# Joint rounding of h and x, three scale instructions moved to ScalarE, and a new VectorE order in a linear-attention + FP4 feed-forward block

## Chip, cores and metric

One core of one Trainium2 chip. The metric is device time in microseconds of one execution (lower is better); the time of a kernel is the median over its runs.

## What is computed

x is (8, 2048, 256), so 16384 tokens of 256 values. With xn = layernorm(x), the output is x + attention(xn) + ffn(xn).

```python
qkv = xn @ W_qkv.T                       # 16 heads of 16
q = softmax(q, axis=-1) * 16 ** -0.5;  k = exp(k)
# buckets of 64 tokens; context and sum of k are cumulated over the buckets before
attn = einsum(q, context) / max(einsum(q, ksum), 1e-6)
attention = attn @ W_out.T

def fp4_quant_dequant(v):                # blocks of 16 along the last axis
    scale = maximum(max(abs(v)) / 6, 1e-12)
    return GRID[searchsorted(MID, abs(v / scale))] * sign(v) * scale
gate = q4(xn) @ q4(w_gate).T;  y = q4(xn) @ q4(w_up).T      # 704 columns
ffn = q4(silu(gate) * y) @ q4(w_down).T
```

## The kernel before, in words

A tile is 128 rows: two buckets of 64 tokens. There are 128 tiles, four sequences of 32. Every engine has its own instruction list, written out by hand, in a function `step(n, d)`: step k = 2n + d does pieces of several tiles at once, and the order of the calls in `step` is the order of the work on that engine. Engines wait for each other, and VectorE for its own results, with counting semaphores (`wait_ge`).

**TensorE** in step k (`step` at the end of its block): the qkv projection of tile k+1; the transpose of attention of k-1; the attention numerator and the context sum (`bucket`) of k; a matmul that subtracts the high half of the attention from its transpose (`less_att`); gate and up of k, first half of the 704 columns (`gate_up(k, 0)`, twelve matmuls of 352 columns); the transpose of xn of k+2 (L1041); six matmuls of `gate_up(k, 1)`; `less_xn` of k+2 (L1049); six more of `gate_up(k, 1)`; the transpose of exp(q) of k+1 (L1073); the output projection of k-2 and the down projection of k-2 (`project_h`, 17 matmuls). `gate_up(k, 1)` writes the PSUM banks in which the qkv product of k+1 stood, so it waits until VectorE has subtracted q's maximum there (`q_shift`) and ScalarE has read k and v (`kv_done`). `less_xn` waits for ScalarE's first copy of the transposed xn (`xnt_split`).

**ScalarE** in step k: first copy of the transposed attention; exp(k) and v of k+1; second copy of the attention; exp(q) of k+1 (`exp_q`, L534, waits for `q_shift`); tanh of the first gate half (L558); first copy of the transposed xn (`split_xnt`, L513); second copy; tanh of the second half; layernorm's normalise of k+3, mean and squares of k+4; copy of the transposed q; eight snapshot copies of the context (L573).

**VectorE** in step k: the last two products of x's quantization for tile k+1 (`scale_x`, L874 and L876, which feed a DMA transpose that SyncE issues); block maxima of x (k+2) and h (k-1); `block_scales` with eleven short instructions, among them two reciprocals, of 16 (x) and 44 (h) block scales, and the high and low halves of the scales; `max_q`; h divided by its scales (`over_scales_h`, L807); `shift_q` (L697); the two residual additions of tile k-3 (`add_up`); between them the three rounding instructions of h (L825, L829, L835) and x's division (L816); the gate products (L734, L744); x's three rounding instructions (L843, L847, L853) spread over the second half; the attention's four short steps (L710, L714, L718, L723); the last two products of h (`scale_h`, L863), which feed the other DMA transpose; `row_factor` (L883, L888). A value is rounded in three instructions: the upper 16 bits of the fp32 quotient with the lowest bit set, a multiplication by a power of two into fp16, and an addition and subtraction on those 16 bits.

h and x have quotient, rounding and scale buffers of their own. POOL computes 1/std of the layernorm. SyncE issues the loads, the stores and the DMA transposes, in a written order (`turn_xq`, `turn_h`, `load`, `store`).

```python
nc.tensor.matmul(tr32, minus16[:, :], xnt[:, par, 0, :], start=False, stop=True, ...)   # less_xn, after
pe.wait_ge(xnt_split, after(t, 2, 1))
...
elif 0 in chunks:                                # gate_up(t, 1)
    pe.wait_ge(q_shift, after(t + 1))
    pe.wait_ge(kv_done, after(t + 1, 3))
```

Of the kernel before, what the change touches and what calls it, by code (L numbers as in the profile page):

```python
# [5 lines left out]
def linear_attention_fp4_ffn_block(nc, x, wqkv_t, wout_t, wgate, wup, wdown, out):  # L6
# [18 lines left out]
    P = 128  # L25
# [41 lines left out]
    with ctx:  # L67
# [74 lines left out]
        xv = sb("xv", [P, D])  # L142
        xw = sb("xw", [P, D], u16)
        xu = sb("xu", [P, D], fp16)
        xq = sb("xq", [P, D], u16)
# [5 lines left out]
        hblk = sb("hblk", [P, 3, FB])  # L151
# [4 lines left out]
        hv = sb("hv", [P, F])  # L156
        hw = sb("hw", [P, F], u16)
        hu = sb("hu", [P, F], fp16)
        hq = sb("hq", [P, F], u16)
# [55 lines left out]
        xq_round = sem("xq_round")  # L215
# [10 lines left out]
        c_row_done = sem("c_row_done")  # L226
        proj_done = sem("proj_done")
# [36 lines left out]
        def _(sp):  # L264
# [35 lines left out]
            def turn_xq(t, par):  # L300
                if not is_tile(t):
                    return
                sp.wait_ge(xq_step, after(t, 8))
                sp.sem_inc(sp_turn, 1)
                if begun(t - 2):
                    sp.wait_ge(gu_done, after(t - 2, 2))
                sp.sem_inc(sp_turn, 1)
                sp.dma_start_transpose(xqt[:, par, :, :].rearrange("p s (c k) -> p (s c) k", k=P),
                                       xq_s[:, par, :, :].rearrange("p s k -> p (s k)")).then_inc(xqt_done[par], 16)

            def turn_h(t, par):
                if not is_tile(t):
                    return
                sp.wait_ge(hq_step, after(t, 14))
# [127 lines left out]
        def _(act):  # L442
# [49 lines left out]
            def normalise_waits(t):  # L492
# [5 lines left out]
                if begun(t - 2):  # L498
                    act.wait_ge(xq_step, after(t - 2, 8, 6))
# [60 lines left out]

            def snapshot(t):
# [14 lines left out]
            def step(n, d):  # L576
# [4 lines left out]
                exp_q(k + 1, odd)  # L581
                tanh_gate(k, 0, par)
# [4 lines left out]
                tanh_gate(k, 1, par)  # L587
                normalise(n, d + 3)
# [41 lines left out]
        def _(dve):  # L630
# [107 lines left out]
            def times_up(t, half, par):  # L738
# [3 lines left out]
                if begun(t - 2):  # L742
                    dve.wait_ge(hq_step, after(t - 2, 14, 8))
# [17 lines left out]
            def block_scales(t, par, u, upar):  # L761

                do_h, do_x = is_tile(t), is_tile(u)
                if do_x:
                    dve.wait_ge(xq_step, after(u, 8, 1))
                    nc.vector.tensor_scalar(xblk[:, 1, :], xblk[:, 0, :], SIX_TIE * 2.0 ** 11, XS * TINY * 2.0 ** 11, ALU.mult, ALU.max)\  # L769
                        .then_inc(xq_step, 1)  # L770
                if do_h:
                    dve.wait_ge(hq_step, after(t, 14, 1))
                    nc.vector.tensor_scalar(hblk[:, 1, :], hblk[:, 0, :], SIX_TIE, h_floor[:, :], ALU.mult, ALU.max)\
                        .then_inc(hq_step, 1)
                if do_x:
                    dve.wait_ge(xq_step, after(u, 8, 2))
                    nc.vector.reciprocal(xblk[:, 2, :], xblk[:, 1, :]).then_inc(xq_step, 1)  # L777
                if do_h:
                    dve.wait_ge(hq_step, after(t, 14, 2))
                    nc.vector.tensor_reduce(hrow[:, 0, :], hblk[:, 1, :], AX.X, ALU.max).then_inc(hq_step, 1)  # L780
                if do_h:
                    nc.vector.reciprocal(hblk[:, 2, :], hblk[:, 1, :]).then_inc(hq_step, 1)
                    dve.wait_ge(hq_step, after(t, 14, 3))
                    nc.vector.tensor_scalar(hrow[:, 1, :], hrow[:, 0, :], 2.0 ** -23, None, ALU.mult)\
                        .then_inc(hq_step, 1)
                if do_x:
                    nc.vector.tensor_copy(xs_hi[:, :].rearrange("p (b i) -> p b i", i=2), twice(xblk[:, 1, :])).then_inc(xq_step, 1)
                if do_h:
                    dve.wait_ge(hq_step, after(t, 14, 5))
                    nc.vector.reciprocal(hrow[:, 2, :], hrow[:, 1, :]).then_inc(hq_step, 1)  # L790
                if do_x:
                    dve.wait_ge(xq_step, after(u, 8, 4))
                    nc.vector.tensor_tensor(xs_lo[:, :].rearrange("p (b i) -> p b i", i=2), twice(xblk[:, 1, :]),
                                            xs_hi[:, :].rearrange("p (b i) -> p b i", i=2), ALU.subtract).then_inc(xq_step, 1)
                if do_h:
                    dve.wait_ge(hq_step, after(t, 14, 6))
                    nc.vector.tensor_scalar(hs_hi[:, :].rearrange("p (b i) -> p b i", i=2), twice(hblk[:, 1, :]), hrow[:, 2, :], None, ALU.mult)\
                        .then_inc(hq_step, 1)

            def over_scales_h(t, par):  # L800
                if not is_tile(t):
                    return
                dve.wait_ge(hq_step, after(t, 14, 4))
                if begun(t - 1):
                    dve.wait_ge(hq_step, after(t - 1, 14, 9))
                rows = lambda ap: ap.rearrange("p (o b i) -> p o b i", b=FB, i=2)
                nc.vector.tensor_tensor(rows(hv[:, :]), rows(h[:, par, :]), pairs_of(hblk[:, 2, :]), ALU.mult)\  # L807
                    .then_inc(hq_step, 1)

            def over_scales_x(t, par):  # L810
                if not is_tile(t):
                    return
                dve.wait_ge(xq_step, after(t, 8, 3))
                if begun(t - 1):
                    dve.wait_ge(xq_round, after(t - 1, 3, 1))
                nc.vector.tensor_tensor(xv[:, :].rearrange("p (o b i) -> p o b i", b=XB, i=2),  # L816
# [3 lines left out]
            def round_h(t, part):  # L820
                if not is_tile(t):
                    return
                if part == 0:
                    dve.wait_ge(hq_step, after(t, 14, 8))
                    nc.vector.tensor_scalar(hw[:, :], hv[:, :].bitcast(u16)[:, 1:2 * F:2], 1, None, ALU.bitwise_or)\  # L825
                        .then_inc(hq_step, 1)
                if part == 1:
                    dve.wait_ge(hq_step, after(t, 14, 9))
                    nc.vector.tensor_scalar(hu[:, :], hw[:, :].bitcast(bf16), 2.0 ** -14, None, ALU.mult)\  # L829
                        .then_inc(hq_step, 1)  # L830
                if part == 2:
                    dve.wait_ge(hq_step, after(t, 14, 10))
                    if begun(t - 1):
                        dve.wait_ge(hq_step, after(t - 1, 14))
                    nc.vector.tensor_scalar(hq[:, :], hu[:, :].bitcast(u16), GRID16, -GRID16, ALU.add, ALU.add)\  # L835
                        .then_inc(hq_step, 1)

            def round_x(t, part):
                if not is_tile(t):
                    return  # L840
                if part == 0:
                    dve.wait_ge(xq_step, after(t, 8, 6))
                    nc.vector.tensor_scalar(xw[:, :], xv[:, :].bitcast(u16)[:, 1:2 * D:2], 1, None, ALU.bitwise_or)\  # L843
                        .then_inc(xq_round, 1)
                if part == 1:
                    dve.wait_ge(xq_round, after(t, 3, 1))
                    nc.vector.tensor_scalar(xu[:, :], xw[:, :].bitcast(bf16), 2.0 ** -3, None, ALU.mult)\  # L847
                        .then_inc(xq_round, 1)
                if part == 2:
                    dve.wait_ge(xq_round, after(t, 3, 2))  # L850
                    if begun(t - 1):
                        dve.wait_ge(xq_step, after(t - 1, 8))
                    nc.vector.tensor_scalar(xq[:, :], xu[:, :].bitcast(u16), GRID16, -GRID16, ALU.add, ALU.add)\  # L853
                        .then_inc(xq_round, 1)

            def scale_h(t, par, part):
# [3 lines left out]
                dve.wait_ge(hq_step, after(t, 14, 12))  # L860
                if begun(t - 2):
                    dve.wait_ge(hqt_done[par], turned(t - 2, par))
                nc.vector.tensor_tensor(rows(hq_s[:, par, part * F:(part + 1) * F]), rows(hq[:, :].bitcast(fp16)),  # L863
                                        over_pairs((hs_hi, hs_lo)[part][:, :]), ALU.mult).then_inc(hq_step, 1)

            def scale_x(t, par):
# [3 lines left out]
                dve.wait_ge(xq_round, after(t, 3))  # L870
                dve.wait_ge(xq_step, after(t, 8, 5))
                if begun(t - 2):
                    dve.wait_ge(xqt_done[par], turned(t - 2, par))
                nc.vector.tensor_tensor(rows(xq_s[:, par, 0, :]), rows(xq[:, :].bitcast(fp16)), over_pairs(xs_hi[:, :]), ALU.mult)\  # L874
                    .then_inc(xq_step, 1)
                nc.vector.tensor_tensor(rows(xq_s[:, par, 1, :]), rows(xq[:, :].bitcast(fp16)), over_pairs(xs_lo[:, :]), ALU.mult)\  # L876
                    .then_inc(xq_step, 1)

            def row_factor(t, par):
                if not is_tile(t):  # L880
                    return
                dve.wait_ge(hq_step, after(t, 14, 7))
                nc.vector.scalar_tensor_tensor(hs_lo[:, :].rearrange("p (b i) -> p b i", i=2), twice(hblk[:, 1, :]), hrow[:, 2, :],  # L883
                                               hs_hi[:, :].rearrange("p (b i) -> p b i", i=2), ALU.mult,
                                               ALU.subtract).then_inc(hq_step, 1)
                if begun(t - 2):
                    dve.wait_ge(o_step, after(t - 2, 2))
                nc.vector.tensor_scalar(c_row[:, par, :], hrow[:, 1, :], c_d[:, :], None, ALU.mult)\  # L888
# [374 lines left out]
```

## Time and profile before

| | |
|---|---|
| median of 3 runs | 1497.29 us (1495.11 to 1497.63) |
| profiled execution, its own time | 1495.11 us |
| its span, first to last instruction | 1493.3 us |
| granted TensorE clock, mean | 0.988 |
| instructions: TensorE / VectorE / ScalarE / POOL | 10702 / 4914 / 3096 / 540 |

The span is read in three parts: about 110 us in which the weights are quantized and transposed and the first steps run, the steady stretch of some 125 steps, and a drain of some 25 us. "Busy" of an engine counts the time in which an instruction of it runs; two neighbours may overlap, since the next one starts before the last one's end. The distance from start to start is therefore what an instruction costs its engine.

### The profile page before, as it was taken

The numbers are of one execution on the slowest core, as the hardware profiler recorded it, in microseconds if no ns is written. First come the engines' busy times: TensorE is split into PE (matmuls) and PEld (weight loads), VectorE is DVE, ScalarE is ACT, GpSimd is POOL, SyncE is SP. The second block draws the span as 40 slices with busy tenths as digits, with TensorE's granted clock in tenths as the row PEclk, the third lists the DMA queues.
The fourth block names the chain that finished last, engine by engine and source line by source line (L and its number), as shares of the span: only waits on it lengthen the run. The fifth ranks groups of instructions, "written<-read, shape, count | busy, mean of one in ns | idle before, by whom it ended". The sixth has DMA issues, their size and how long they took to land.

```text
span 1493.3 us, 43457 instructions
## 1 busy us (share of the span) xinstructions
PE 1382.8 (93%) x10702; PEld 948.7 (64%) x10702; DVE 1434.4 (96%) x4914; ACT 1011.0 (68%) x3096; POOL 175.8 (12%) x540
## 2 busy tenths in 40 slices
PE   0259999999999999999999999999999999999997
PEld 0136666666666666666666666666666666666664
DVE  5859999999999999999999999999999999999997
ACT  1687767676767677676767676767767676767662
POOL 1520101010101101010101010110101010101000
PEclk9969999999999999999999999999999999999998
DMA  5002233333332333333333323333333333233324
GB/s 114 4 7 55 63 65 77 69 63 74 70 76 58 81 68 70 64 81 68 63 71 74 72 58 78 68 70 64 81 68 69 65 77 71 61 73 70 71 47 78
DMA packets 293241, 100.01 MB, mean 67 GB/s; under 512 B 258272, under 2 KB 292704, under 8 KB 293216
## 3 DMA queue, kind: packets, MB, share of 16 engines
q1 hardware_dynamic: 293216, 99.73, 31.8%
q8 instruction: 9, 0.15, 0.0%
q14 instruction: 16, 0.13, 0.0%
HBM read 19.99 MB, written 16.78 MB: 25 GB/s over the span
## 4 chain that ended last, share of the span: by engine, by line
DVE 53%; issue 34%; DVEq 7%; ACT 3%; PE 1%; SPq 1%; DMA 0%; POOL 0%; ACTq 0%; POOLq 0%
DVE q_rows L863 5%; DVE osum L900 4%; DVE hw L825 4%; DVE xblk L758 3%; DVE h L744 3%; DVE xw L843 2%; DVE hu L829 2%; DVE hq L835 2%; DVE hv L807 2%; DVE xq_s L876 2%; DVE att L723 1%; DVE xblk L777 1%; DVE qsh L697 1%; DVE hs_lo L883 1%; DVE xblk L769 1%
## 5 line engine op out<-in xcount | busy, mean ns | idle before, releaser
L1154 PE MATMUL outp<-w_down_cat,q_rows 128*128 128x256 f16 x1408 | 246.2, 274 | 0.0
L573 ACT ACTIVATE snap<-ctxp,mask 64x68 f32<-64x68 f32 x1024 | 236.2, 308 | 3.2
L550 ACT ACTIVATE att_t<-trp 128x256 f16<-128x256 f32 x256 | 98.3, 384 | 134.0 <-PE trp L1109 129.6
L534 ACT ACTIVATE qexp<-qsh,c_q 128x256 f32<-128x256 f32 x128 | 65.1, 508 | 147.4 <-DVE qsh L697 147.3
L398 POOL TENSOR_TENSOR var_scaled<-squares,var_mul 128x1 f32<-128x1 f32 x128 | 24.8, 194 | 1188.4 <-ACT scratch L488 1181.7
L1154 PEld LDWEIGHTS outp<-w_down_cat,q_rows 128*128 128x128 f16 x1408 | 138.3, 98 | 16.5
L1156 PE MATMUL outp<-w_down_lo,q_rows 128*128 128x256 f16 x640 | 147.6, 274 | 0.0
L513 ACT ACTIVATE xnt<-trp 128x256 f16<-128x256 f32 x256 | 96.8, 378 | 57.3 <-PE trp L1049 57.3
L751 DVE TENSOR_REDUCE hblk<-h 128x44 f32<-128x704 f32 x128 | 123.6, 966 | 0.1
L807 DVE TENSOR_TENSOR hv<-h,hblk 128x704 f32<-128x704 f32 x128 | 112.7, 881 | 0.0
L558 ACT ACTIVATE th<-unit1a,c_g 128x352 f32<-128x352 f32 x128 | 69.7, 545 | 36.3 <-PE unit1b L1027 36.3
L1087 PE MATMUL nump<-snap,qt 128*64 128x144 f32 x1024 | 91.0, 299 | 3.2 <-ACT snap L573 3.2
L558 ACT ACTIVATE th<-unit0a,c_g 128x352 f32<-128x352 f32 x128 | 69.8, 545 | 29.7 <-PE unit0b L1027 29.7
L1041 PE MATMUL trp<-ident,xn 128*128 128x128 f32 x256 | 49.4, 275 | 37.7 <-ACT xn L504 37.7
L1023 PE MATMUL unit0a<-w_gate,xqt 128*128 128x352 f16 x256 | 80.5, 315 | 3.4 <-DVE qsh L697 1.2
L1023 PE MATMUL unit1a<-w_gate,xqt 128*128 128x352 f16 x256 | 80.5, 314 | 2.9
L504 ACT ACTIVATE xn<-xring,shift,rstd 128x256 f32 (+1 forms) x128 | 75.3, 589 | 11.1 <-POOL shift L408 11.1
L1023 PE MATMUL unit1b<-w_up,xqt 128*128 128x352 f16 x256 | 80.0, 313 | 0.0
L1025 PE MATMUL unit1b<-w_up,xqt 128*128 128x352 f16 x256 | 80.0, 313 | 0.0
L1023 PE MATMUL unit0b<-w_up,xqt 128*128 128x352 f16 x256 | 80.0, 313 | 0.0
L1027 PE MATMUL unit1b<-w_up,xqt 128*128 128x352 f16 x256 | 80.0, 313 | 0.0
L1027 PE MATMUL unit0a<-w_gate,xqt 128*128 128x352 f16 x256 | 80.0, 313 | 0.0
(214 smaller groups left out, 4409.2 us busy)
## 6 DMA issues: line engine op xcount, KB each, us to landing
xring<-x SPq DMA_DIRECT2D x128, 128.0 KB, 2.7
out<-xring SPq DMA_DIRECT2D x128, 128.0 KB, 2.5
xqt<-xq_s SPq DMA_TRANSPOSE x128, 2.4
q_rows<-q_rows SPq DMA_TRANSPOSE x128, 3.5
raw_qkv<-wqkv_t SPq DMA_DIRECT2D x1, 768.0 KB, 7.7
raw_gate<-wgate SPq DMA_DIRECT2D x8, 88.0 KB
raw_up<-wup SPq DMA_DIRECT2D x8, 88.0 KB
raw_down<-wdown SPq DMA_DIRECT2D x1, 704.0 KB, 6.2
```

Of the source, the lines that this page charges most:

```text
L513: nc.scalar.activation(xnt[:, par, part, :], tr32, ACT.Copy).then_inc(xnt_split, 1)
L550: nc.scalar.activation(att_t[:, par, part, :], tr32, ACT.Copy).then_inc(att_split, 1)
L558: nc.scalar.activation(th[:, half, :], unit[(par + half) % 2][0][:, 0:FH], ACT.Tanh, scale=c_g[:, :])\
L573: nc.scalar.activation(kept[:, :, cols], sums[:, :, cols], ACT.Copy, scale=mask[rows, f, h:h + 1])\
L751: nc.vector.tensor_reduce(hblk[:, 0, :], h[:, par, :].rearrange("p (o b i) -> p b o i", b=FB, i=2), AX.XY, ALU.max, apply_absolute_value=T ...
L807: nc.vector.tensor_tensor(rows(hv[:, :]), rows(h[:, par, :]), pairs_of(hblk[:, 2, :]), ALU.mult)\
L1023: nc.tensor.matmul(o, stat_hi, m, start=first, stop=False)
L1025: nc.tensor.matmul(o, stat_hi, m, start=False, stop=False)
L1027: end = nc.tensor.matmul(o, stat_lo, m, start=False, stop=last)
L1087: last = nc.tensor.matmul(nump[rows, g * 2 * SW:(g + 1) * 2 * SW], qt[:, par, g * P + s * BUCKET:g * P + (s + 1) * BUCKET], snap[:, g, s, ...
L1154: nc.tensor.matmul(downp, hqt[:, par, m, :], w_down_cat[:, m, :], start=(m == 0), stop=False)
L1156: nc.tensor.matmul(downp, hqt[:, par, m, :], w_down_lo[:, m, :], start=False, stop=False)
```

## The change

The scale, quotient and rounding buffers of h and x are laid side by side (`blk` of 44 + 16 columns, `hx_v`, `hx_w`, `hx_u`, `hx_q` of 704 + 256), so that one reciprocal and three rounding instructions serve both. The powers of two in h's scales are changed so that one factor fits both. The high halves of both scales (`xs_hi`, `hs_hi`) and the row factor (`c_row`) are computed on ScalarE: the first two between `exp_q` and the first `tanh_gate`, the last behind the second `tanh_gate`. On VectorE, `max_q` moves ahead of the row maximum and the reciprocal, `shift_q` ahead of the row scale's reciprocal and h's division, and x's division stands directly behind h's.

```diff
-        xblk = sb("xblk", [P, 3, XB])
+        blk = sb("blk", [P, 3, FB + XB])
+        hblk, xblk = blk[:, :, 0:FB], blk[:, :, FB:FB + XB]
...
+            def scales_x(t):                       # ScalarE
+                act.wait_ge(xq_step, after(t, 6, 2))
+                nc.scalar.activation(xs_hi[:, :].rearrange("p (b i) -> p b i", i=2), twice(xblk[:, 1, :]), ACT.Copy)\
+                    .then_inc(x_scaled, 1)
+            def factor_of_row(t, par):
+                act.wait_ge(hq_step, after(t, 9, 4))
+                if begun(t - 2):
+                    act.wait_ge(o_step, after(t - 2, 2))
+                nc.scalar.activation(c_row[:, par, :], hrow[:, 1, :], ACT.Copy, scale=c_d[:, :]).then_inc(c_row_done, 1)
+            def scales_h(t):
+                act.wait_ge(hq_step, after(t, 9, 5))
+                nc.scalar.activation(hs_hi[:, :].rearrange("p (b i) -> p b i", i=2), twice(hblk[:, 1, :]), ACT.Copy,
+                                     scale=hrow[:, 2, :]).then_inc(h_scaled, 1)
...
                 exp_q(k + 1, odd)
+                scales_x(k + 2)
+                scales_h(k - 1)
                 tanh_gate(k, 0, par)
...
                 tanh_gate(k, 1, par)
+                factor_of_row(k - 1, odd)
                 normalise(n, d + 3)
...
+            def over_one(t, u):                    # VectorE: row maximum, joined reciprocal
+                    nc.vector.tensor_reduce(hrow[:, 0, :], hblk[:, 1, :], AX.X, ALU.max).then_inc(hq_step, 1)
+                    nc.vector.reciprocal(blk[:, 2, both], blk[:, 1, both]).then_inc(hx_step, 1)
+            def round_hx(t, u, part):
+                both = slice(0 if do_h else F, F + D if do_x else F)
+                if part == 0:
+                        dve.wait_ge(hq_step, after(t, 9, 6))
+                        dve.wait_ge(xq_step, after(u, 6, 3))
+                    nc.vector.tensor_scalar(hx_w[:, both], hx_v[:, both].bitcast(u16)[:, 1:2 * (both.stop - both.start):2], 1, None,
+                                            ALU.bitwise_or).then_inc(hx_step, 1)
...
+            def low_scales(t, u):                  # waits for x_scaled and h_scaled, then xs_lo and hs_lo
...
                 block_max_h(k - 1, odd)
-                block_scales(k - 1, odd, k + 2, par)
+                block_scales(k - 1, k + 2)
                 max_q(k + 1, odd)
+                over_one(k - 1, k + 2)
+                row_scale(k - 1)
+                shift_q(k + 1, odd)
+                over_row(k - 1)
                 over_scales_h(k - 1, odd)
-                shift_q(k + 1, odd)
+                over_scales_x(k + 2, par)
+                round_hx(k - 1, k + 2, 0)
                 add_up(n, d - 3, 0)
-                round_h(k - 1, 0)
-                over_scales_x(k + 2, par)
-                round_h(k - 1, 1)
+                round_hx(k - 1, k + 2, 1)
                 add_up(n, d - 3, 1)
-                round_h(k - 1, 2)
+                round_hx(k - 1, k + 2, 2)
                 gate_h(k, 0, par)
-                row_factor(k - 1, odd)
-                round_x(k + 2, 0)
+                low_scales(k - 1, k + 2)
                 times_up(k, 0, par)
-                round_x(k + 2, 1)
                 attention(k, par, 0)
                 scale_h(k - 1, odd, 0)
+                attention(k, par, 1)
                 scale_h(k - 1, odd, 1)
-                round_x(k + 2, 2)
-                attention(k, par, 1)
                 attention(k, par, 2)
```

`row_scale` also waits for `c_row_done` of the tile before, because ScalarE now reads `hrow`. The rows that ScalarE and SyncE wait for are renumbered; SyncE's order is the same.

## Rows read from the trace of the kernel before

**Rows 1.** Steady stretch: busy us (xcount) of PE, PEld, DVE, ACT, POOL; clock, DMA, GB/s.
```profile
200.00:1450.00 1250.00, 1236.78 (x9604) 849.42 (x9602) 1244.39 (x4407) 874.18 (x2779) 131.59 (x460) 1.00 0.33 70
```

**Rows 2.** VectorE groups by shape, 200 to 1450 us: count, busy us, mean ns, idle.
```profile
L807 DVE TENSOR_TENSOR hv<-h,hblk 128x704 f32<-128x704 f32 x116 | 102.2, 881 | 0.0
L825 DVE TENSOR_SCALAR hw<-hv 128x704 uint16<-128x704 uint16 x116 | 59.6, 514 | 0.0
L782 DVE RECIPROCAL hblk<-hblk 128x44 f32<-128x44 f32 x116 | 48.5, 418 | 0.0
L829 DVE TENSOR_SCALAR hu<-hw 128x704 f16<-128x704 bf16 x116 | 38.7, 334 | 0.0
L843 DVE TENSOR_SCALAR xw<-xv 128x256 uint16<-128x256 uint16 x116 | 32.4, 279 | 0.0
L797 DVE TENSOR_SCALAR hs_hi<-hblk,hrow 128x88 bf16<-128x88 f32 x116 | 30.9, 266 | 0.0
L777 DVE RECIPROCAL xblk<-xblk 128x16 f32<-128x16 f32 x116 | 28.5, 246 | 0.0
L847 DVE TENSOR_SCALAR xu<-xw 128x256 f16<-128x256 bf16 x116 | 25.1, 217 | 0.0
L888 DVE TENSOR_SCALAR c_row<-hrow,c_d 128x1 f32<-128x1 f32 x116 | 23.7, 204 | 0.0
L787 DVE CAST xs_hi<-xblk 128x32 bf16<-128x32 f32 x116 | 20.0, 172 | 0.0
```

**Rows 3.** VectorE in one step, in order of time: start us, duration us, engine, line.
```profile
813.75 0.42 DVE L697 TENSOR_TENSOR qsh<-unit1b,qmax 128x256 f32<-128x256 f32 x1
814.08 0.47 DVE L900 SCALAR_TENSOR_TENSOR osum<-outp,c_o,xring 128x256 f32<-128x256 f32 x1
...
818.77 0.16 DVE L714 SCALAR_TENSOR_TENSOR dmx<-dz,nump 128x16 f32<-128x16 f32 x1
818.96 0.25 DVE L718 RECIPROCAL drec<-dmx 128x16 f32<-128x16 f32 x1
```

**Rows 4.** TensorE in the same step, in order of time.
```profile
808.57 0.39 PE L1023 MATMUL unit1a<-w_qkv,xnt 128*128 128x512 f16 x1
...
810.53 0.38 PE L1109 MATMUL trp<-ident,att 128*128 128x128 f32 x2
...
813.86 0.38 PE L1041 MATMUL trp<-ident,xn 128*128 128x128 f32 x2
814.30 0.32 PE L1023 MATMUL unit1a<-w_gate,xqt 128*128 128x352 f16 x1
...
815.05 0.31 PE L1027 MATMUL unit1b<-w_up,xqt 128*128 128x352 f16 x1
815.48 0.28 PE L1049 MATMUL trp<-xnt,minus 128*128 128x256 f16 x1
...
816.50 0.38 PE L1073 MATMUL trp<-ident,qexp 128*128 128x128 f32 x2
816.71 0.27 PE L1023 MATMUL outp<-w_out,att_t 128*128 128x256 f16 x1
...
819.42 0.39 PE L1023 MATMUL unit0a<-w_qkv,xnt 128*128 128x512 f16 x1
```

**Rows 5.** ScalarE in the same step, in order of time.
```profile
812.60 0.38 ACT L550 ACTIVATE att_t<-trp 128x256 f16<-128x256 f32 x1
814.20 0.51 ACT L534 ACTIVATE qexp<-qsh,c_q 128x256 f32<-128x256 f32 x1 [1.22 <-DVE qsh L697]
814.62 0.53 ACT L558 ACTIVATE th<-unit0a,c_g 128x352 f32<-128x352 f32 x1
815.05 0.37 ACT L513 ACTIVATE xnt<-trp 128x256 f16<-128x256 f32 x1
...
816.77 0.56 ACT L558 ACTIVATE th<-unit1a,c_g 128x352 f32<-128x352 f32 x1 [0.53 <-PE unit1b L1027]
...
819.02 1.87 ACT L573 ACTIVATE snap<-ctxp,mask 64x68 f32<-64x68 f32 x8
```

More of the change, by code:

```diff
@@ L788, in block_scales @@
[L788 to L798, printed above, removed]
+            def over_row(t):
+                if not is_tile(t):
+                    return
+                dve.wait_ge(hq_step, after(t, 9, 4))
+                nc.vector.reciprocal(hrow[:, 2, :], hrow[:, 1, :]).then_inc(hq_step, 1)
@@ L859, in scale_h @@
                 rows = lambda ap: ap.rearrange("p (o c) -> p o c", c=2 * FB)
[L860 to L863, printed above, removed]
+                if part == 0:
+                    dve.wait_ge(hx_step, hx_after(t + 3, 4))
+                    if begun(t - 2):
+                        dve.wait_ge(hqt_done[par], turned(t - 2, par))
+                else:
+                    dve.wait_ge(hq_step, after(t, 9, 7))
+                nc.vector.tensor_tensor(rows(hq_s[:, par, part * F:(part + 1) * F]), rows(hx_q[:, 0:F].bitcast(fp16)),
                                         over_pairs((hs_hi, hs_lo)[part][:, :]), ALU.mult).then_inc(hq_step, 1)
@@ L869, in scale_x @@
                 rows = lambda ap: ap.rearrange("p (o c) -> p o c", c=2 * XB)
-                dve.wait_ge(xq_round, after(t, 3))
-                dve.wait_ge(xq_step, after(t, 8, 5))
+                dve.wait_ge(hx_step, hx_after(t, 4))
+                dve.wait_ge(xq_step, after(t, 6, 4))
                 if begun(t - 2):
                     dve.wait_ge(xqt_done[par], turned(t - 2, par))
-                nc.vector.tensor_tensor(rows(xq_s[:, par, 0, :]), rows(xq[:, :].bitcast(fp16)), over_pairs(xs_hi[:, :]), ALU.mult)\
+                nc.vector.tensor_tensor(rows(xq_s[:, par, 0, :]), rows(hx_q[:, F:F + D].bitcast(fp16)), over_pairs(xs_hi[:, :]), ALU.mult)\
@@ L875, in scale_x @@
                     .then_inc(xq_step, 1)
-                nc.vector.tensor_tensor(rows(xq_s[:, par, 1, :]), rows(xq[:, :].bitcast(fp16)), over_pairs(xs_lo[:, :]), ALU.mult)\
+                nc.vector.tensor_tensor(rows(xq_s[:, par, 1, :]), rows(hx_q[:, F:F + D].bitcast(fp16)), over_pairs(xs_lo[:, :]), ALU.mult)\
                     .then_inc(xq_step, 1)
[L879 to L888, printed above, removed]
-                    .then_inc(c_row_done, 1)
+            def low_scales(t, u):
+                if is_tile(u):
+                    dve.wait_ge(x_scaled, after(u))
+                    nc.vector.tensor_tensor(xs_lo[:, :].rearrange("p (b i) -> p b i", i=2), twice(xblk[:, 1, :]),
+                                            xs_hi[:, :].rearrange("p (b i) -> p b i", i=2), ALU.subtract).then_inc(xq_step, 1)
+                if is_tile(t):
+                    dve.wait_ge(h_scaled, after(t))
+                    nc.vector.scalar_tensor_tensor(hs_lo[:, :].rearrange("p (b i) -> p b i", i=2), twice(hblk[:, 1, :]), hrow[:, 2, :],
+                                                   hs_hi[:, :].rearrange("p (b i) -> p b i", i=2), ALU.mult,
+                                                   ALU.subtract).then_inc(hq_step, 1)
```

126 lines of the change are left out of this document (56 added, 70 removed).

## The prediction

> **What bounds the kernel now.** I read the busy times by stretch first. Between 200 and 1450 us VectorE is busy 1244 of 1250 us, TensorE 1237 at a granted clock of 1.00 (its level of 2.4 GHz), ScalarE 874 [rows 1]. The reader should see two full engines, not one. Next come VectorE's groups: each stands there 116 times [rows 2], so a step takes 1250 / 116 = 10.78 us, and no group has idle time before it. VectorE is the bound. TensorE's busy time is misleading, since durations overlap; its slack has to be found in the distances from start to start.
>
> So the third view is the timeline of TensorE for one step, 808.57 to 819.42, 10.85 us [rows 4]. It has two places in which more time passes than the work needs. (a) The transpose of xn starts at 813.86 and the next matmul, first of `gate_up(k, 1)`, at 814.30: 0.44 us. The same pair of transposes followed by an fp16 matmul takes 0.21 at 816.50. The wait in between is for `shift_q`, which ends at 813.75 + 0.42 = 814.17 [rows 3]. (b) Six gate matmuls run from 814.30, five distances of (815.05 - 814.30) / 5 = 0.15; `less_xn` should follow 0.15 behind the last, but starts 0.43 behind it, at 815.48. ScalarE's copy that it waits for ends at 815.05 + 0.37 = 815.42 [rows 5]. So 0.23 + 0.28 = 0.51 of this step is waiting, and TensorE's own step is 10.85 - 0.51 = **10.34 us**. I looked at some eighty steps: both waits are in every one, smaller in the neighbouring step, which is also shorter. Both go back to VectorE: (a) directly, (b) because ScalarE's exp(q) waited 1.22 us for the same `shift_q`, and tanh and the copy stand behind it [rows 5].
>
> The timeline is therefore: VectorE 10.78, TensorE 10.34 close behind it, ScalarE 874 / 116 = 7.5. Whatever VectorE loses beyond 0.44 us a step cannot show.
>
> **The change, part by part: VectorE.** An independent instruction starts before its predecessor ends: L697 takes 0.42 and the next starts 0.33 behind it, so an instruction costs its duration less 0.09. One that needs the result right in front of it costs more: L714 takes 0.16 and L718 starts 0.19 behind it [rows 3], 0.12 above the rule.
> - Moved to ScalarE: `xs_hi` 172 ns, `hs_hi` 266, `c_row` 204 [rows 2]. 0.64 - 3 x 0.09 = 0.37 us saved.
> - Reciprocals: 418 ns for 44 columns, 246 for 16, so 6.1 ns a column; 60 columns take 418 + 98 = 516. Two cost 0.66 - 0.18 = 0.48, one 0.43: 0.05 saved.
> - First rounding instruction: 514 ns for 704 columns, 279 for 256, 0.52 a column; 960 columns take 649. 0.61 becomes 0.56: 0.05. The second: 334 and 217, so 401 for 960; 0.37 becomes 0.31: 0.06. The third, of the same width on 16-bit data, I price like the second: 0.06.
> - L718 gets h's second product between it and L714: 0.12 saved. But the joined first rounding stands directly behind x's division, whose result it needs: 0.12 lost. The other moved instructions each keep a neighbour between them and their source.
> Sum: 0.37 + 0.05 + 0.05 + 0.06 + 0.06 = **0.59 us saved**; VectorE then needs 10.78 - 0.59 = 10.19 a step. Bounds: the joined instructions could save nothing (0.37), or each save the whole fixed part, about 0.2 as the 16-column reciprocal suggests, instead of 0.05 (1.0). I keep the slopes, since both widths of each form are in the trace.
>
> **TensorE.** `shift_q` now stands ahead of h's division (881 - 90 = 0.79) and the high scales are out (0.08 + 0.18), so relative to the rest of the step it ends at least 1.05 earlier, at 813.1 instead of 814.17. Gap (a) closes whole: `gate_up(k, 1)` could start at 814.07. Bounds of (a): 0.21 left as at 816.50, or all of 0.44 as now, if the other waits of that call or the change from fp32 to fp16 cost it. I take 0.21, because that row is the same pair of instructions followed by an fp16 matmul.
>
> **ScalarE**, in offsets from TensorE's first matmul of the step (808.57). Its second attention copy is done at 4.41 (812.60 + 0.38). exp(q) started at 5.63 and can now start at about 4.6; it holds the engine 0.42 (814.20 to 814.62), so until 5.0. The two new copies, 32 and 88 columns wide, have no row of their own; the nearest are the snapshot copies, 68 columns with a per-partition scale, 1.87 / 8 = 0.23 each [rows 5]. Two end at 5.47. The bounds are 0.2 and 0.8 for the two. tanh cannot start before the gate is in PSUM anyway: the second half's starts 0.27 behind the first transpose that follows the gate (816.50 to 816.77), so the first half's can start at 5.29 + 0.27 = 5.56 at the earliest. **The copies fit into that wait, with 0.09 to spare.** Then tanh 0.43, the xn copy 0.37, done at 6.36; the matmul starts 0.06 later (815.42 to 815.48), at 6.42. TensorE is there at 5.29 + 0.21 + 6 x 0.15 = 6.40. Of (b) 0.02 stays. If the copies took 0.8 instead of 0.47, 0.24 more would stay.
>
> The ScalarE page of the Trainium skill, "ScalarE: Activation LUTs", section "Rules for kernel authors", speaks against this move: simple multiplications belong on VectorE, which is faster by the element. In the same page's figures (186 ns and 0.833 a column, 93 more for a scale read from memory, 93 of overlap) I estimate 0.12 and 0.26 for the two copies, 0.38 in all, and the stay of (b) would be as above, 0.02. The rule is about the cost of one operation; here the operation goes where there is a wait.
>
> The row factor behind the second tanh costs about 0.2 in front of normalise. ScalarE's step, counted to the end of the snapshots, ended 820.89, 1.47 into TensorE's next step; with the shorter step and the extra work it ends at about 1.7, before the numerator matmuls behind the transpose at 810.53 - 808.57 = 1.96 need it. `c_row` of a tile is used two steps later, and VectorE's wait for it before the next row scale is some 5 us behind it. `low_scales` waits for copies done at 5.5, and comes at about 7. I cost these at nothing; the cover of the low scales is 1.5 us.
>
> **Who waits now.** TensorE's step is 10.34 + 0.02 = 10.36, VectorE's 10.19. VectorE runs ahead until `max_q` has to wait for the qkv product, which ends at about 2.1; that is its new idle place, 0.17 a step. POOL, SyncE and the DMA transposes keep their order and their slack.
>
> **Sum.** 10.78 - 10.36 = 0.42 us, in 125 steps: 52 us. The drain has no x and little TensorE work; there VectorE saves the moved instructions, 0.37 in three steps: 1 us. The start is kept. The profiled execution, 1495.1 (span 1493.3 and 1.8 around it), becomes 1442; it is 2.2 below the median of the runs shown, so a median is some 2 us above that. I give **1443 us**.
>
> **The rivals.**
> 1. *Gap (a) is not VectorE's* (0.14). It stays at 0.44. TensorE's step is 10.59, 0.19 saved, 24 us: 1471. For it: the call has two more waits than the one at 816.71. Against it: the matmul starts 0.13 behind `shift_q`'s end, as one that was released by it would.
> 2. *TensorE is no floor* (0.04). Then all of VectorE's 0.59 shows: 125 x 0.59 = 74, so 1421. Against it: the matmuls stand 0.15 apart with no wait between them. The page "TensorE: Matmul & The Clock Gate", section "Back-to-back issue gap", would have it so: it gives 131 ns for a matmul of 512 columns in a sustained stream of weight loads and matmuls. The trace disagrees: 0.15 for 352 columns. By that page TensorE would have room and the time would be the 1421 of this rival.
> 3. *ScalarE's copies come late* (0.06, the slower side). Place: between exp(q) and the first tanh. Each 0.1 us in which they hold tanh beyond 5.56 delays `less_xn`, and so the step, by 0.1. The point at which it decides is a step of 10.78, so copies (with their wait for the reciprocal of the row scale, which stands behind `shift_q`) of 0.47 + 0.09 + 0.42 = 0.98 us. At 1.3 us the step is 11.1: 125 x 0.32 = 40 slower, 1537. Against: no row of ScalarE shows a short copy above 0.31, and the reciprocal is done 0.25 behind `shift_q`, while exp(q) runs.
> 4. *Nothing changes* (0.03): VectorE meets new waits on ScalarE, as long as what it saves. 1497. Against: 1.5 us of cover.
> 5. *As forecast* (0.73), 1434 to 1454: 0.1 us of a step either way is 12 us.
>
> **How the numbers follow.** The likeliest case gives 1443. The range reaches down to 1431 (the gap behind the transpose shrinks to the plain distance of 0.15, 7 us, and a little of the start) and up to 1473, which takes in rival 1, and copies at their bound of 0.8 us (0.24 a step, 30 us: also 1473); it leaves out rivals 2, 3 and 4, 0.13 together, and what lies beyond their neighbours' bounds. A measurement of this kernel tells 0.2%, 3 us, from no change. Faster: cases 5, 1, 2, less a little, 0.91; the same 0.03; slower 0.06.
>
> **What would show it.** Right: VectorE has idle time in front of `max_q`, released by the qkv matmuls, of about 0.17 us a step; TensorE's distance behind the xn transpose is 0.21 and in front of `less_xn` about 0.17; exp(q) starts right behind the attention copy and waits no more; the step is 10.36. Wrong: `less_xn` still 0.3 or more behind its predecessor with ScalarE as releaser (rival 3), the 0.44 kept with `shift_q` long done (rival 1), VectorE without idle time (I mis-sized it).

## The result, and the profile after

| | before | changed |
|---|---|---|
| median | 1497.39 us (4 runs, 1495.11 to 1497.63) | 1443.53 us (4 runs, 1442.89 to 1445.99) |
| ratio | | 0.9644, 95% interval 0.963 to 0.9659 |
| span of the profiled execution | 1493.3 | 1441.8 |

Forecast were 1443 and a range of 1431 to 1473. The busy times in the steady stretch of the changed kernel, the row that answers to [rows 1]:

```profile
200.00:1400.00 1200.00, 1200.00 (x9600) 856.04 (x9599) 1163.06 (x3595) 936.88 (x3125) 135.32 (x460) 1.00 0.34 73
```

TensorE is busy all of the 1200 us, VectorE 1163. A step takes 1200 / 116 = 10.345 us; it took 10.78. (Averaged from start to start over more than 100 steps: 10.355, and 10.784 before. The difference of 0.43 is the same.) The chain of work that ended last was mostly VectorE and "issue" before; now the page of the profile gives it to TensorE:

```profile
PE 91%; ACT 3%; DVE 2%; issue 1%; ACTq 0%; DVEq 0%
```

TensorE in one step of the changed kernel, in order of time, the rows that answer to [rows 4]:

```profile
805.80 0.39 PE L1032 MATMUL unit1a<-w_qkv,xnt 128*128 128x512 f16 x1
...
807.76 0.38 PE L1118 MATMUL trp<-ident,att 128*128 128x128 f32 x2
...
811.09 0.38 PE L1050 MATMUL trp<-ident,xn 128*128 128x128 f32 x2
811.31 0.31 PE L1032 MATMUL unit1a<-w_gate,xqt 128*128 128x352 f16 x1
...
812.05 0.31 PE L1036 MATMUL unit1b<-w_up,xqt 128*128 128x352 f16 x1
812.25 0.28 PE L1058 MATMUL trp<-xnt,minus 128*128 128x256 f16 x1
...
815.98 0.28 PE L1166 MATMUL outp<-w_down_lo,q_rows 64*128 64x256 f16 x1
816.20 0.39 PE L1032 MATMUL unit0a<-w_qkv,xnt 128*128 128x512 f16 x1
```

The gap behind the transpose of xn (811.09 to 811.31) is 0.22; it was 0.44. The one in front of the subtraction (812.05 to 812.25) is 0.20 here and 0.15 in the neighbouring step; 0.43 and 0.32 before. On average over all steps the first went from 0.44 to 0.22 and the second from 0.37 to 0.175.

ScalarE in the same step, the answer to [rows 5], with the two new copies (L563, L578) and the row factor (L572):

```profile
809.83 0.38 ACT L548 ACTIVATE att_t<-trp 128x256 f16<-128x256 f32 x1
810.11 0.50 ACT L532 ACTIVATE qexp<-qsh,c_q 128x256 f32<-128x256 f32 x1
810.51 0.22 ACT L563 ACTIVATE xs_hi<-blk 128x32 bf16<-128x32 f32 x1
810.63 0.36 ACT L578 ACTIVATE hs_hi<-blk,hrow 128x88 bf16<-128x88 f32 x1
811.37 0.55 ACT L556 ACTIVATE th<-unit0a,c_g 128x352 f32<-128x352 f32 x1 [0.38 <-PE unit0b L1036]
811.82 0.38 ACT L511 ACTIVATE xnt<-trp 128x256 f16<-128x256 f32 x1
...
814.00 0.28 ACT L572 ACTIVATE c_row<-hrow,c_d 128x1 f32<-128x1 f32 x1
```

exp(q) follows the attention copy at once; it waited 1.22 us. tanh still waits, now for the gate matmuls, 0.38 us behind the copies.

VectorE's waits and groups, 200 to 1400 us (first the view of waits: total, times, longest; then groups):

```profile
DVE qmax L711 <- PE unit0b L1036: 20.7, 58, 0.4
DVE qmax L711 <- PE unit1b L1036: 10.3, 55, 0.3
```
```profile
L848 DVE TENSOR_SCALAR hx_w<-hx_v 128x960 uint16<-128x960 uint16 x116 | 76.5, 660 | 4.0
L806 DVE RECIPROCAL blk<-blk 128x60 f32<-128x60 f32 x116 | 60.0, 517 | 0.0
L757 DVE SCALAR_TENSOR_TENSOR ga<-th,unit0a 128x352 f32<-128x352 f32 x116 | 56.2, 485 | 0.0
L852 DVE TENSOR_SCALAR hx_u<-hx_w 128x960 f16<-128x960 bf16 x116 | 46.3, 399 | 0.0
L860 DVE TENSOR_SCALAR hx_q<-hx_u 128x960 uint16<-128x960 uint16 x116 | 46.2, 398 | 0.0
```

VectorE is now idle in front of `max_q`, released by the qkv matmuls, as forecast, and for longer: 31.0 / 116 = 0.27 us a step by this view. By distances it is 0.35, because `max_q` usually starts 0.08 to 0.09 before its predecessor ends: the distance in front of it averages 0.51, where without a wait it is 0.16 (experiments 2 and 7). So VectorE's own need, the time that its instructions of one step take when it waits for no other engine, is 10.345 - 0.35 = **9.99 us**, TensorE's **10.345**. Its slack, what it can lose before the step gets longer, is the 0.35. (With the averaged step it is 10.355 - 0.35 = 10.00. The expectations use 9.99 and 10.345.)

### The profile page after: what moved, and what is told of

Its sections match the earlier page's. It is cut to its first block, busy times and chain, and to the rows that moved or that the text cites. A ratio compares the mean times of both kernels' runs of the same rounds, so it can differ in the third digit from the quotient of the medians.

```text
span 1441.8 us, 42471 instructions
## 1 busy us (share of the span) xinstructions
PE 1342.2 (93%) x10702; PEld 955.3 (66%) x10702; DVE 1342.9 (93%) x4030; ACT 1081.1 (75%) x3480; POOL 179.9 (12%) x540
## 4 chain that ended last, share of the span: by engine, by line
PE 91%; ACT 3%; DVE 2%; issue 1%; ACTq 0%; DVEq 0%
PE outp L1163 11%; PE nump L1096 6%; PE unit1a L1032 5%; PE unit0a L1032 5%; PE outp L1165 5%; PE unit1a L1034 5%; PE unit1a L1036 5%; PE unit0a L1034 4%; PE unit0a L1036 4%; PE ctxp L1106 4%; PE unit1b L1034 4%; PE unit1b L1032 4%; PE unit1b L1036 4%; PE unit0b L1036 4%; PE unit0b L1032 4%; PE unit0b L1034 4%
## 5 line engine op out<-in xcount | busy, mean ns | idle before, releaser
L396 POOL TENSOR_TENSOR var_scaled<-squares,var_mul 128x1 f32<-128x1 f32 x128 | 34.4, 269 | 1134.0 <-ACT scratch L486 1126.3
L774 DVE TENSOR_REDUCE blk<-h 128x44 f32<-128x704 f32 x128 | 123.8, 968 | 0.1
L827 DVE TENSOR_TENSOR hx_v<-h,blk 128x704 f32<-128x704 f32 x128 | 111.5, 871 | 0.0
L848 DVE TENSOR_SCALAR hx_w<-hx_v 128x960 uint16<-128x960 uint16 (+2 forms) x131 | 84.9, 648 | 4.9
L1034 PE MATMUL unit1b<-w_up,xqt 128*128 128x352 f16 x256 | 80.0, 313 | 0.0
L1036 PE MATMUL unit0b<-w_up,xqt 128*128 128x352 f16 x256 | 80.0, 313 | 0.0
L1032 PE MATMUL unit0b<-w_up,xqt 128*128 128x352 f16 x256 | 80.0, 313 | 0.0
L1034 PE MATMUL unit0b<-w_up,xqt 128*128 128x352 f16 x256 | 80.0, 313 | 0.0
```

The source lines that it names most:

```text
L774: nc.vector.tensor_reduce(hblk[:, 0, :], h[:, par, :].rearrange("p (o b i) -> p b o i", b=FB, i=2), AX.XY, ALU.max, apply_absolute_value=T ...
L827: nc.vector.tensor_tensor(rows(hx_v[:, 0:F]), rows(h[:, par, :]), pairs_of(hblk[:, 2, :]), ALU.mult)\
L1032: nc.tensor.matmul(o, stat_hi, m, start=first, stop=False)
L1034: nc.tensor.matmul(o, stat_hi, m, start=False, stop=False)
L1036: end = nc.tensor.matmul(o, stat_lo, m, start=False, stop=last)
```

## The experiments

Theory A, the prediction's, sharpened by that profile: a step takes the larger of TensorE's 10.345 and VectorE's need, and the change lowers the second from 10.78 to 9.99. Rivals: B, the early subtraction of q is what ends TensorE's waits; C, the other parts are each needed; D, TensorE is no bound; E, VectorE still is the bound; F, ScalarE's copies are on the path.

**1. q late, rest kept.**

```diff
-                max_q(k + 1, odd)
                 over_one(k - 1, k + 2)
                 row_scale(k - 1)
-                shift_q(k + 1, odd)
+                max_q(k + 1, odd)
                 over_row(k - 1)
                 over_scales_h(k - 1, odd)
+                shift_q(k + 1, odd)
```

> The changed kernel with q's maximum and subtraction put back where they stood (maximum behind the row scale, subtraction behind h's division); everything else of the change stays. Theory A (VectorE now has 0.27 us of idle time a step and TensorE is the bound, so the order of q is no longer needed): 1443 to 1446 us, TensorE's step still 10.35. q's subtraction ends 0.3 us later in TensorE's step, still before ScalarE is free for exp(q). Theory B (the early subtraction is what ends TensorE's waits): both waits come back, 0.1 to 0.3 us a step, 1455 to 1480.

Measured: 1443.77 us (1442.95 to 1447.02). Theory B falls: both of TensorE's gaps are as in the changed kernel, 0.22 and 0.175 on average. With VectorE below TensorE's need it is ahead by itself, and q's subtraction is early enough at either place.

**2. Scales and row factor back on VectorE.**

```diff
-                scales_x(k + 2)                    # ScalarE
-                scales_h(k - 1)
...
-                factor_of_row(k - 1, odd)
...
                 row_scale(k - 1)                   # VectorE
+                high_x(k + 2)
                 shift_q(k + 1, odd)
...
+                high_h(k - 1)
                 gate_h(k, 0, par)
                 low_scales(k - 1, k + 2)
+                factor_of_row(k - 1, odd)
```

> The changed kernel with the three scale instructions back on VectorE (0.09 + 0.19 + 0.12 = 0.40 us a step); joined rounding and q's order stay. Theory A: VectorE needs 10.07 + 0.40 = 10.47 us a step, over TensorE's 10.35, becomes the bound again, and the time rises by 0.12 x 125 = 15 us to 1459 (1450 to 1470). Theory C (the gain is in the order and the joined instructions): no change, 1443.

Measured: 1444.14 us (1444.1 to 1446.52). This is the number that C, as the expectation words it, had; A's missed by 15 us. I had set VectorE's need from the idle time (0.27), not from the distance (0.35). With 9.99 + 0.38 = 10.37 it is level with TensorE: its step averages 10.38, and it has no wait in front of `max_q` any more. Taken alone, the run cannot tell A, so corrected, from C; experiments 3, 4 and 5 do. In VectorE's timeline the three instructions cost 0.09, 0.17 and 0.12 (806.71 to 806.80, 810.44 to 810.61, 811.37 to 811.49):

```profile
806.71 0.17 DVE L866 CAST xs_hi<-blk 128x32 bf16<-128x32 f32 x1
806.80 0.42 DVE L695 TENSOR_TENSOR qsh<-unit1b,qmax 128x256 f32<-128x256 f32 x1
...
810.44 0.26 DVE L871 TENSOR_SCALAR hs_hi<-blk,hrow 128x88 bf16<-128x88 f32 x1
810.61 0.52 DVE L732 SCALAR_TENSOR_TENSOR ga<-th,unit0a 128x352 f32<-128x352 f32 x1
...
811.37 0.21 DVE L878 TENSOR_SCALAR c_row<-hrow,c_d 128x1 f32<-128x1 f32 x1
811.49 0.51 DVE L742 TENSOR_TENSOR h<-ga,unit0b 128x352 f32<-128x352 f32 x1
```

**3. Not joined.**

```diff
-                    nc.vector.reciprocal(blk[:, 2, both], blk[:, 1, both]).then_inc(hx_step, 1)
+                    for s in parts:                # slice(0, FB), slice(FB, FB + XB)
+                        nc.vector.reciprocal(blk[:, 2, s], blk[:, 1, s]).then_inc(hx_step, 2 // len(parts))
...
```
The three rounding instructions are parted in the same way, with the waits in front of them unchanged.

> The changed kernel with separate instructions for h and x in the reciprocal and the three rounding steps (same places). By the slopes VectorE pays 0.06 + 3 x 0.06 = 0.25 us more a step, and gets 0.12 back, since x's division no longer stands directly in front of an instruction that needs it. Theory A: 0.13 fits into the idle 0.27, so 1443 to 1445. Theory C (the joining is needed): 0.25 a step, 1470.

Measured: 1444.02 us (1442.83 to 1444.88), as A had it. The 0.12 that the expectation gave back did not come: this kernel still waits for x's division in front of the first rounding instruction of h, and the distance behind that division is 0.45, as in the changed kernel. By distances the parting costs 0.22, and 9.99 + 0.22 still lies below TensorE's step.

**4. Only the moves to ScalarE** (edits 1 and 3 together).

> Of the change only the three instructions moved to ScalarE (and the places of x's rounding and the attention's short steps): separate instructions for h and x, q's maximum and subtraction late as before. Theory A: VectorE needs 10.2 to 10.35 us a step, at or below TensorE's 10.35: 1443 to 1450. Theory B or C (the other parts carry the gain): 1465 or more.

Measured: 1444.74 us (1444.56 to 1447.78). One part of the change gives its whole time, to within some 1 us. The buffers' new layout and the new places are still in this kernel; the three moves on the otherwise unchanged kernel before were not run.

**5. Only the order** (edits 2 and 3 together).

> The changed kernel with both other parts undone: the three scale instructions on VectorE and separate instructions for h and x; q's early subtraction and the new places stay. Counted in distances from start to start, VectorE needs 9.99 us a step in the changed kernel (10.345 less 0.35 in front of q's maximum). Theory A (VectorE's need against TensorE's 10.345): 9.99 + 0.38 + 0.26 - 0.12 = 10.51, so 0.165 x 125 = 21 us more, 1464 (1455 to 1475). Theory B (q's early subtraction is what ends TensorE's waits): 1444 to 1450.

Measured: 1473.21 us (1470.51 to 1474.83). Theory A's 1464 is 9 us off, inside its range. Now VectorE is over the line. The step below takes 10.54, read between the same instruction in two steps,

```profile
804.33 0.73 DVE L826 TENSOR_SCALAR hx_w<-hx_v 128x704 uint16<-128x704 uint16 x2
...
814.42 0.41 DVE L810 TENSOR_TENSOR hx_v<-xn,blk 128x256 f32<-128x256 f32 x1
814.87 0.53 DVE L826 TENSOR_SCALAR hx_w<-hx_v 128x704 uint16<-128x704 uint16 x1
```

but the steps differ, and over 105 of them the average is 10.60. That is 0.245 above the changed kernel's 10.355; 125 x 0.245 = 31, and 29.7 were measured. The expectation's 10.51 was short by the 0.12 that it gave back, as in experiment 3: the distance behind x's division is 0.45 here too (814.42 to 814.87). By distances the scale instructions cost 0.38 and the parting 0.22: 10.00 + 0.60 = 10.60. TensorE's gap behind the transpose of xn stays closed (0.22); it waits in front of the output projection instead (0.34 on average, where the changed kernel has 0.11). Theory B falls a second time: here q is early, and 30 us of the gain are gone.

**6. The kernel before, with q early and nothing else.**

```diff
-                block_scales(k - 1, odd, k + 2, par)
                 max_q(k + 1, odd)
-                over_scales_h(k - 1, odd)
+                block_scales(k - 1, odd, k + 2, par)
                 shift_q(k + 1, odd)
+                over_scales_h(k - 1, odd)
```

> The kernel before with nothing changed but q: its maximum ahead of the block scales, its subtraction ahead of h's division. Theory A: VectorE stays the bound at 10.78 less up to 0.1 us (one or two short waits between the scale instructions get a neighbour), 1485 to 1497; TensorE's two waits at the old places shrink and turn up at another place. Theory B: 1450 to 1470.

Measured: 1490.63 us (1488.84 to 1491.72), ratio 0.9964 (0.995 to 0.9977). It is worth 5 us, by the waits that it covers on VectorE: its step falls from 10.78 to 10.74. TensorE's gap behind the transpose of xn did close, from 0.44 to 0.24 on average. But TensorE has to stay in step with VectorE, and most of that wait turned up in front of the output projection, whose PSUM is free only when VectorE's residual addition has read it: 0.28 on average, where the kernel before has 0.11, and 0.43 in this step.

```profile
802.56 0.38 PE L1073 MATMUL trp<-ident,qexp 128*128 128x128 f32 x2
802.99 0.27 PE L1023 MATMUL outp<-w_out,att_t 128*128 128x256 f16 x1
```

The wait in front of the subtraction hardly changed (third row below, 200 to 1350 us: 43.7 / 108 = 0.40 us; the same view has 48.7 / 116 = 0.42 for the kernel before and 23.8 / 116 = 0.21 for the changed one), and ScalarE's for q's subtraction is still there too. The last row is the wait in front of the output projection, which the view gives in every other step:

```profile
ACT qexp L534 <- DVE qsh L697: 104.7, 107, 1.0
ACT xnt L513 <- PE trp L1049: 48.2, 108, 0.5
PEld trp L1049 <- ACT xnt L513: 43.7, 108, 0.4
PEld outp L1023 <- DVE xring L905: 10.1, 53, 0.2
```
(For TensorE the view counts the time in which no weights are loaded, so 0.2 of its row is there without any wait.) An engine that is not the bound has to wait somewhere in each step. Where it waits depends on the order in which the bound does its work; the releaser says where the wait showed, not what makes it.

**7. TensorE relieved**: the six matmuls of w_down's low half are left out. (The `.then_inc(proj_done, 1)` on the last matmul stays and is not shown.)

```diff
-                    nc.tensor.matmul(downp, hqt[:, par, m, :], w_down_cat[:, m, :], start=(m == 0), stop=False)
-                    if m < FC:
-                        nc.tensor.matmul(downp, hqt[:, par, m, :], w_down_lo[:, m, :], start=False, stop=False)
-                nc.tensor.matmul(downp, hqt[0:FR, par, FC, :], w_down_lo[0:FR, FC, :], start=False, stop=True)
+                    last = nc.tensor.matmul(downp, hqt[:, par, m, :], w_down_cat[:, m, :], start=(m == 0), stop=(m == HT - 1))
```

> The changed kernel without the six matmuls of the down projection's low weight half (left out: the low half of w_down). It takes 5 x 0.109 + 0.21 = 0.75 us a step off TensorE, to 9.59. Theory A: VectorE becomes the bound with its own need of 9.99 us (the prediction's sum had 10.19): 1443.5 - 0.355 x 125 = 1399; at 10.19 it would be 1424. Theory D (TensorE is no bound): 1443.

Measured: 1399.34 us (1398.33 to 1402.72). The step falls to VectorE's own need and no further: 115 steps between 200 and 1350 us, 10.0 us each.

```profile
L827 DVE TENSOR_TENSOR hx_v<-h,blk 128x704 f32<-128x704 f32 x115 | 100.4, 873 | 0.0
```

This settles VectorE's need at 10.00 (10.005 from start to start) and shows my sum of 10.19 wrong; and it shows TensorE as the bound of the changed kernel (D falls). TensorE's wait in front of the subtraction is back, 0.43 on average, although q is early here.

**8. More work for VectorE.**

```diff
+                    for i in range(4):
+                        nc.vector.reciprocal(more[:, i, :, :], dmx[:, :, :])
                     nc.vector.reciprocal(drec[:, :, :], dmx[:, :, :]).then_inc(att_step, 1)
```

> The changed kernel with four more 16-column reciprocals on VectorE in each step (same input as the attention's reciprocal, results unused), 4 x 0.16 = 0.64 us a step. Theory A: 0.35 of it fits into the idle time in front of q's maximum; the other 0.29 shows, 36 us, 1480. Theory E (VectorE is still the bound, its idle time only apparent): 0.64 x 128 = 82 us, 1525.

Measured: 1457.34 us (1455.89 to 1459.3). Both numbers missed, A's by 23 us, because the four cost less than I took:

```profile
811.70 0.58 DVE L743 RECIPROCAL more<-dmx 128x16 f32<-128x16 f32 x4
812.20 0.20 DVE L744 RECIPROCAL drec<-dmx 128x16 f32<-128x16 f32 x1
812.31 0.46 DVE L760 SCALAR_TENSOR_TENSOR ga<-th,unit0a 128x352 f32<-128x352 f32 x1
```

From 811.70 to 812.31 it is 0.61; the one reciprocal took 0.16 there in the changed kernel. 0.45 more, less the 0.35 of slack, is 0.10, 13 us; measured 14. Theory A holds with the trace's own price.

**9 and 10. ScalarE's copies twice, three times.**

```diff
                 act.wait_ge(xq_step, after(t, 6, 2))
+                for i in range(1):                 # 2 in the other kernel; the same for hs_hi
+                    nc.scalar.activation(more_x[:, i, :].rearrange("p (b i) -> p b i", i=2), twice(xblk[:, 1, :]), ACT.Copy)
```

> The changed kernel with the two scale copies on ScalarE each issued twice (the extra ones into unused tiles), 0.12 + 0.26 = 0.38 us more between exp(q) and the first tanh. Theory A (the copies lie in ScalarE's wait for the gate matmuls, 0.38 to 0.39 us idle before that tanh now): 1443 to 1447. Theory F (ScalarE's work there is on the path): 0.38 x 125 = 47 us, 1490.

Measured: 1444.82 us (1444.52 to 1445.65), as A had it; F falls.

> The same with each copy issued three times, 0.76 us more. Theory A: the first 0.38 is covered, the rest delays tanh, the copy of xn and TensorE's subtraction one for one: 0.37 x 125 = 46 us, 1490 (1480 to 1495), with ScalarE as the releaser in front of the subtraction. That is rival 3 of the prediction at a price of 1.14 us. If ScalarE is not on any path: 1444.

Measured: 1476.6 us (1475.75 to 1478.01): the doubled copies were still covered and the tripled ones are not, as expected, but the price is 33 us, not 46. The copies push tanh to 808.47; the gate is ready 0.27 behind the transpose's start (807.92), at 808.19:

```profile
807.34 0.34 ACT L566 ACTIVATE more_x<-blk 128x32 bf16<-128x32 f32 x2
807.58 0.21 ACT L567 ACTIVATE xs_hi<-blk 128x32 bf16<-128x32 f32 x1
807.70 0.61 ACT L583 ACTIVATE more_h<-blk,hrow 128x88 bf16<-128x88 f32 x2
808.22 0.35 ACT L585 ACTIVATE hs_hi<-blk,hrow 128x88 bf16<-128x88 f32 x1
808.47 0.54 ACT L558 ACTIVATE th<-unit0a,c_g 128x352 f32<-128x352 f32 x1
```
```profile
807.92 0.38 PE L1057 MATMUL trp<-ident,xn 128*128 128x128 f32 x2
...
808.88 0.31 PE L1043 MATMUL unit1b<-w_up,xqt 128*128 128x352 f16 x1
809.33 0.28 PE L1065 MATMUL trp<-xnt,minus 128*128 128x256 f16 x1
```

tanh is 0.28 late and the subtraction stands 0.45 behind its predecessor. On average over the steps it is 0.42, 0.25 more than in the changed kernel; 125 x 0.25 = 31. ScalarE's copy is its releaser in the view of waits, as expected. The slack was again 0.1 larger than the idle time: by distances 0.47, where the trace shows 0.38 idle. This is rival 3's mechanism, brought about by added work.

**11. The last matmul over 128 rows.** In every step TensorE has 0.21 in front of the one 64-row matmul and 0.21 behind it (815.98 to 816.20 above).

```diff
+            nc.vector.memset(w_down_lo[FR:P, FC, :], 0.0).then_inc(low_zero, 1)
...
-                nc.tensor.matmul(downp, hqt[0:FR, par, FC, :], w_down_lo[0:FR, FC, :], start=False, stop=True)\
+                nc.tensor.matmul(downp, hqt[:, par, FC, :], w_down_lo[:, FC, :], start=False, stop=True)\
...
+            pe.wait_ge(low_zero, 1)
```

> The changed kernel with the last matmul of the down projection over all 128 rows instead of 64; the other 64 weight rows are zero, so the product is the same. In the trace the distance in front of the 64-row matmul is 0.21 and behind it 0.21, where 128-row neighbours of the same width stand 0.109 apart. Theory A (TensorE's matmul distances are the bound): 0.2 us a step less if both distances become 0.11, 1443.5 - 25 = 1418; 0.1 less, 1431, if only one does. VectorE's 9.99 is still below. Theory D (TensorE is no bound): 1443.

Measured: **1418.34 us** (1417.56 to 1421.44), as expected: the matmul uses more rows of the array, and the time is shorter. A step averages 10.15, 0.21 less; both distances are 0.109 in every step. 128 rows against 64 is the only difference inside a step.

**12. The same, with xn's copy ahead of tanh.**

```diff
-                tanh_gate(k, 0, par)
                 split_xnt(k + 2, par, 0)
+                tanh_gate(k, 0, par)
```

> The same, and on ScalarE the first copy of the transposed xn ahead of the first tanh instead of behind it. TensorE's subtraction of xn waits 0.05 us in every other step in the changed kernel; that wait goes: 3 us below full_rows. The first gate product on VectorE gets its tanh 0.4 us later; if that has no slack, up to 0.1 us a step is lost, 12 us above full_rows.

Measured: **1414.1 us** (1412.36 to 1414.55), ratio to the kernel before 0.9448 (0.9435 to 0.9461). This is 4 us below experiment 11, where 3 were expected, and below both kernels. A step averages 10.115, and the gap in front of the subtraction is now 0.15 in every step; the later tanh cost nothing that shows. TensorE's distances around the subtraction and the last matmul:

```profile
806.60 0.31 PE L1038 MATMUL unit0b<-w_up,xqt 128*128 128x352 f16 x1
806.75 0.27 PE L1060 MATMUL trp<-xnt,minus 128*128 128x256 f16 x1
...
810.37 0.27 PE L1168 MATMUL outp<-w_down_lo,q_rows 128*128 128x256 f16 x1
810.48 0.38 PE L1034 MATMUL unit1a<-w_qkv,xnt 128*128 128x512 f16 x1
```

## Why the prediction was right, and what was off in it

- **The bound changes.** Forecast: TensorE's own step 10.34, with the stay of the second wait 10.36; measured 10.345 (10.355 from start to start). This carries the number 1443. That it came out to within 1 us is partly luck, since 0.01 us in the step is 1.25 us. Experiments 7, 8 and 11 show the bound from three sides: less work on TensorE helps down to VectorE's need, more on VectorE costs only past the slack, and the time follows TensorE's distances.
- **Gap (a)** closes to 0.22 (taken: 0.21). Rival 1 falls. The reason given for it was not the one that counts (see below).
- **Gap (b)** keeps 0.03 on average (0.175 against 0.15; taken: 0.02). exp(q) starts at 4.31 in TensorE's step, where I had 4.6, since the engine's overlap and VectorE's lead both help.
- **The copies on ScalarE** take 0.38 from 810.51 to 810.51 + 0.12 + 0.26; I took 0.47 from the snapshot row. The estimate by the Trainium skill's page "ScalarE: Activation LUTs", section "What ACT_TABLE_LOAD costs", was 0.38, and the trace agrees (218 ns for 32 columns, 356 for 88 with a scale from memory, both means of 115 or more; 0.12 and 0.26 from start to start in experiments 9 and 10). The rule of that page's section "Rules for kernel authors" against simple multiplications on this engine did not decide anything here: the place was a wait. Experiment 9 shows that even twice the work there is free, 10 that three times is not.
- **VectorE's sum was mis-sized**: 0.59 forecast, 0.78 measured. By distances, averaged over more than 100 steps of either kernel, the moved instructions gave 0.43 and not 0.37, the joined ones 0.26 and not 0.22, the two exchanged waits 0 as forecast; another 0.06 came from the second gate product, for which no saving was forecast, and 0.03 is spread over several short distances. The durations of the joined forms were 517, 660, 399 and 398 ns, against 516, 649, 401 and 401. It cost nothing, since TensorE's step hid all of it beyond 0.43. By the same error I gave VectorE an idle 0.17 us a step; it was 0.35.
- **What I had not said**: that the parts replace each other. I priced the early q at the closing of TensorE's waits; experiment 1 shows that they close without it, once VectorE's need is not above TensorE's 10.35. VectorE had to lose 0.43 a step, the change takes off 0.78, and the moves alone (experiment 4, with the new places and buffers kept) suffice. In the prediction the earlier end of `shift_q` was the reason given for gap (a). On the kernel before, it does close that gap (experiment 6), but the wait turns up elsewhere and 5 us are gained; the reason for the shorter step is that VectorE no longer sets the pace. The prediction held because its sum also compared the two engines' steps.
- **Rival 2 and the page on matmul spacing.** In the changed kernel the distances stayed at 0.15 for 352 columns in a stream without a wait, and the step ended on them, so rival 2 falls. The figure of 131 ns for 512 columns in a sustained stream, from the Trainium skill's page "TensorE: Matmul & The Clock Gate", section "Back-to-back issue gap", would have had rival 2; the trace has 216 ns for 512 columns. The measurement decides. The section's other formula, columns / 2.4 + 2.5 ns, which it gives for a single matmul, is what this stream shows: 216, 149 and 109 ns for 512, 352 and 256 columns.
- **Rivals 3 and 4** did not occur: 0.03 is left in front of the subtraction, and VectorE's only wait for another engine between 200 and 1400 us is the forecast one.

## What to carry to other kernels

Before summing what an edit saves on the busiest engine, find the next engine's own step from its start-to-start distances: here VectorE was relieved of 0.78 us a step, of which only 0.43 could show, and the moves without joining and early q, or joining and early q without the moves, reached that point. A wait on the second engine that is released by the first is a symptom of the pace, so moving its releaser ahead helps little while the pace stays (5 us here). When the bound has moved, the next edit has to be on the new bound: one 64-row matmul made into 128 rows gave 25 us, nearly half as much as the whole change.

## What the runs showed that I had not expected

- The 64-row matmul cost more than the same one over 128 rows: 0.42 us for the two distances around it, 0.22 with zeros in the other 64 rows. Why was not tried. In the steady stretch the two distances are the same in every step.
- An engine's idle time in the trace understates its slack by the overlap of neighbours, 0.08 to 0.1 us on VectorE and ScalarE; it is most of the 15 and of the 13 us by which experiments 2 and 10 missed.
- Of the 16-column reciprocals that follow each other without a wait, the first costs 0.16 us and each further one 0.11.
- The second gate product on VectorE takes 0.46 us in the changed kernel and 0.52 in most steps before, with the same operands; the first takes 0.51 in both. It took 0.46 in every run that has the new buffers, whatever else was undone, and 0.52 in both that have the old ones. Why was not tried.
